# First stage of a six-stage transformer kernel: the order of the next batch's turns and projections among the scan's units

## The reference

```python
# layer 1: linear attention, 16 heads of 32
q, k, v = heads(x @ q_w.T + q_b), heads(x @ k_w.T + k_b), heads(x @ v_w.T + v_b)
qp, kp = elu(q) + 1.0, elu(k) + 1.0
kv = einsum('bhsd,bhse->bhde', kp, v)
z = einsum('bhsd,bhd->bhs', qp, kp.sum(axis=2))[..., None]
attn = einsum('bhsd,bhde->bhse', qp, kv) / (z + EPS)
x = layernorm(x + (attn.reshape(...) @ o_w.T + o_b))
# layer 2: a selective scan over ctx (4 x 512 x 256), gated by silu(x)
u = silu(causal_conv4(einsum('bld,ed->bel', ctx, in_proj_w)) + conv_b)
dt_low, Bm, Cm = split(x_proj_w @ u)              # 16, 16, 16 rows
dt = softplus(dt_proj_w @ dt_low + dt_proj_b)
state = state * exp(dt * A) + (dt * u) * Bm       # 512 steps, 16 states
y = (sum(state * Cm) + D * u) * silu(x)
x = layernorm(x + y)
```

## Time and profile before

| what | value |
|---|---|
| median of 3 runs | 2933.25 us (2930.64 to 2933.45) |
| profiled execution | 2924.15 us |
| its span, first to last instruction | 2922.5 us |
| mean granted clock of PE over the span | 0.947 |
| PE busy | 2622.4 us (90%) |
| DVE busy | 2023.4 us (69%) |
| ACT busy | 1172.5 us (40%) |
| POOL busy | 650.1 us (22%) |
| stage 1 | until about 843 us |

### The profile page before, as it was taken

How to read it: one execution, slowest core, us unless ns; L and a number is a source line. 1 busy time by engine, 2 the same in 40 slices (tenths; PEclk the granted TensorE clock), 3 DMA queues, 4 the chain that set the end, 5 groups by cost and what they waited for, 6 DMA issues and landing times. The chain is left out here.

```text
span 2922.5 us, 29347 instructions
## 1 busy us (share of the span) xinstructions
PE 2622.4 (90%) x9682; PEld 1657.0 (57%) x9682; DVE 2023.4 (69%) x4017; ACT 1172.5 (40%) x2107; POOL 650.1 (22%) x569
## 2 busy tenths in 40 slices
PE   5687897998979889799989999999999998999998
PEld 2233343343448655466656665666666665588886
DVE  2779889789885557688876888578867887222232
ACT  3343363444443222255544555355544555121111
POOL 0544445345411145311101111011101110000000
PEclk9898998999979999899999999999999999999999
DMA  4111112111221102333233223232222314300000
GB/s 143 36 59 51 58 45 79 44 44 65 80 79 58 65 29 87 114 101 101 93 97 114 79 77 91 83 116 75 82 84 89 109 45 127 121 0 30 29 15 15
DMA packets 90785, 212.46 MB, mean 73 GB/s; under 512 B 9990, under 2 KB 34822, under 8 KB 86540
## 3 DMA queue, kind: packets, MB, share of 16 engines
q1 hardware_dynamic: 81324, 178.26, 18.8%
q0 software_dynamic: 5472, 21.01, 1.9%
q10 hardware_dynamic: 3840, 11.34, 1.1%
HBM read 164.11 MB, written 46.47 MB: 72 GB/s over the span
## 5 line engine op out<-in xcount | busy, mean ns | idle before, releaser
L2104 POOL TENSOR_TENSOR h<-du,Bb 128x1024 f32<-128x1024 f32 x128 | 310.2, 2425 | 300.8 <-DVE h L1667 286.9
L1662 DVE TENSOR_TENSOR_SCAN h<-bank,h 128x512 f32<-128x512 f32 x256 | 299.4, 1206 | 25.8 <-ACT bank L1267 18.7
L1267 ACT ACTIVATE bank<-dt,A 128x512 f32<-128x512 f32 x256 | 174.6, 690 | 327.5 <-DVE h L1662 325.0
L1438 ACT ACTIVATE p<-bank,sm,rq 128x512 f32<-128x512 f32 x256 | 199.2, 778 | 243.5 <-DVE sm L2019 243.5
L2182 POOL TENSOR_TENSOR rq<-rq,mhalf 128x4 f32<-128x4 f32 x64 | 69.5, 1085 | 797.0 <-DVE rq L1973 797.0
L637 PE MATMUL bank<-pT,v 128*128 128x512 f32 x512 | 233.0, 598 | 2.8 <-ACT pT L1158 2.8
L251 POOL TENSOR_SCALAR rstd<-mv 128x1 f32<-128x1 f32 x96 | 29.0, 302 | 925.0 <-DVE mv L245 925.0
L637 PE MATMUL bank<-kr,q 128*128 128x512 f32 x512 | 232.9, 598 | 0.0
L837 PE MATMUL bank<-h,ident 128*128 128x512 f32 x256 | 157.3, 699 | 80.6 <-DVE h L1667 80.5
L962 PE MATMUL bank<-x_hi,wxq_s 128*128 128x512 f32 x512 | 189.5, 452 | 6.6 <-DVE x_lo L1994 6.6
L1929 DVE COPY_PREDICATED val<-msk,val 128x258 f32<-128x258 int32 x448 | 173.8, 451 | 28.2 <-DVE val L1929 0.5
(11 more groups left out here) (239 smaller groups left out, 5560.6 us busy)
## 6 DMA issues: line engine op xcount, KB each, us to landing
wxq_s<-wq_dram SPq DMA_DIRECT2D x48, 512.0 KB, 4.4
Bb<-bc_dram SPq DMA_DIRECT2D x32, 512.0 KB, 3.5
Cb<-bc_dram SPq DMA_DIRECT2D x32, 512.0 KB, 3.6
x_dram<-xo POOLq DMA_DIRECT2D x16, 1024.0 KB, 4.7
xc<-x_dram SPq DMA_DIRECT2D x16, 1024.0 KB, 5.3
woh<-in_Wo SPq DMA_DIRECT2D x64, 256.0 KB, 2.6
wxv_s<-wkv_dram SPq DMA_DIRECT2D x12, 1024.0 KB, 5.4
wxk_s<-wkv_dram SPq DMA_DIRECT2D x12, 1024.0 KB, 7.5
```

What stands on the lines that cost most here:

```text
L1267: act.activation(bank[2 + n][:, :], dt[:, c % 2, et, :], ACT.Exp, scale=A[:, et, 2 * w + n:2 * w + n + 1]).then_inc(dA_ready, 1)
L1438: act.activation(p4[:, t, :], bank[4 + t][:, :], ACT.Exp, bias=sm4[:, 4 + t:5 + t], scale=rq[:, hh % 2, 1, t:t + 1], accum_out=sm4[:, 8 + ...
L1662: dve.tensor_tensor_scan(h[:, s, n, :], bank[2 + n][:, :], h[:, s, n, :], 0.0, ALU.mult, ALU.add).then_inc(scanned, 1)
L2104: pool.tensor_tensor(h[:, G % HR, :, :], du[:, et:et + 1, :].to_broadcast([P, 2, S]), Bb[:, w % 2, :, :], ALU.mult).then_inc(dBu_ready, 1)
```

## The change

In stage 1 only:

1. `turn_x` of the next batch moves from slots 30 and 31 to slots 15, 17 and 18, since attended values now stay in `er` (written in place) and no longer take `xT`. The first three `values` of the next batch go to slots 29 to 31, the fourth to slot 1; for batch 0 the first three are computed before the first scan, ahead of `in_xdbl(0)`.
2. `keys` move from slots 3 to 6 to slots 2, 3, 4 and 6; `in_project` goes from two at slot 7 and two at slot 12 to one each at slots 5, 7, 9 and 11, `queries` from slots 13 to 16 to slots 8, 10, 12 and 14. DVE's `conv`, `key`, `query` follow.
3. `keys_values` moves from slot 18 to 13, `in_xdbl` from 17 to 16, `normalisers` from 19 to 17, `turn_normalisers` from 20 to 18, and `in_dt`, `spread`, `attend`, `project_out`, `first`, `last` one slot earlier. POOL's `ln_pool` of the first norm goes from units 30, 31, 0, 1 to units 29, 30, 31, 0.
4. ACT: `value` copies follow the new order (two of them in the n == 0 place of units 0 and 1), `gate_x1` moves from unit 0 of the next batch to unit 31.

```diff
         list0(*[("in", 0, n) for n in range(KI)], *[("x", 0, k) for k in range(KD)], *[("q", 0, n) for n in range(KD)],
-              ("xdbl", 0), *[("dt", 0, n) for n in range(KI)])
+              ("v", 0, 0), ("v", 0, 1), ("v", 0, 2), ("xdbl", 0), *[("dt", 0, n) for n in range(KI)])
...
+            list0(("kv", c, 0), ("kv", c, 1))
+            if c:
+                list0(("q", c, 3))
             if more:
+                list0(("x", c + 1, 0), ("x", c + 1, 1), ("xdbl", c + 1))
+            list0(("z", c))
...
-                group(d[:, :], [(attnT[:, k, t * P:(t + 1) * P], wo[:, k, :]) for k in range(KD)] + [(pick[:, 2, :], rows[:, :])], bank_full)
+                group(d[:, :], [(er[:, k // 2, k % 2, t * P:(t + 1) * P], wo[:, k, :]) for k in range(KD)] + [(pick[:, 2, :], rows[:, :])], bank_full)
...
             for n in range(KD):
                 queries(0, n)
+            pe.wait_ge(rows_ready, START + 1)
+            for t in range(3):
+                values(0, t)
             in_xdbl(0)
...
+                    if U == 1:
+                        values(c, 3)
+                    if U in (2, 3, 4):
+                        keys(c, U - 2)
+                    if U == 6:
+                        keys(c, 3)
+                    if U in (5, 7, 9, 11) and more:
+                        in_project(c + 1, (U - 5) // 2)
+                    if U in (8, 10, 12, 14) and c:
+                        queries(c, (U - 8) // 2)
+                    if U == 13:
+                        keys_values(c)
+                    if U == 15 and more:
+                        turn_x(c + 1, 0)
+                        turn_x(c + 1, 1)
+                    if U == 16 and more:
                         in_xdbl(c + 1)
+                    if U == 17:
+                        normalisers(c)
+                        if more:
+                            turn_x(c + 1, 2)
                     if U == 18:
                         turn_normalisers(c)
+                        if more:
+                            turn_x(c + 1, 3)
...
+                    if U in range(29, 32) and more:
+                        values(c + 1, U - 29)
...
-            gate_x1(B - 1)
+                            if U == 31:
+                                if more:
+                                    value(c + 1, 0)
+                                gate_x1(c)
...
-                    if U in (30, 31):
-                        ln_pool(pool, after(c, 8, U - 30), U % 2)
-                    if U in (0, 1) and c:
-                        ln_pool(pool, after(c - 1, 8, 2 + U), U % 2)
+                    if U in (29, 30, 31):
+                        ln_pool(pool, after(c, 8, U - 29), (U - 29) % 2)
+                    if U == 0 and c:
+                        ln_pool(pool, after(c - 1, 8, 3), 1)
```

More of the change, by code:

```diff
@@ L186, in build @@
             if more:
-                list0(*[("x", c + 1, k) for k in range(KD)])
+                list0(("v", c + 1, 0), ("v", c + 1, 1), ("v", c + 1, 2))
         list0(*[("yt", B - 1, t) for t in range(NT)])
@@ L801, in _ @@
                             pe.matmul(bank[4 + et][:, :], diagD[:, et, :], u[:, et, :], start=True, stop=False)
[L802 to L811, removed]
@@ L831, in _ @@
-                    if U in (30, 31) and more:
-                        turn_x(c + 1, 2 * U - 60)
-                        turn_x(c + 1, 2 * U - 59)
+                        if more:
+                            turn_x(c + 1, 3)
+                    if U in (19, 20) and more:
+                        in_dt(c + 1, 2 * U - 38)
+                        in_dt(c + 1, 2 * U - 37)
+                    if U in (21, 22):
+                        spread(c, 2 * U - 42)
+                        spread(c, 2 * U - 41)
@@ L1190, in key, with value @@
             def key(c, t):
-                if c and t == 0:
-                    act.wait_ge(*FREED["at", c - 1, 2])
-                    act.wait_ge(*FREED["at", c - 1, 3])
                 exp_relu(8 * c + t + (0 if c else 4), ("k", c, t), 0.0, 0.0)
+            def value(c, t):
+                d, free = full("v", c, t)
+                act.activation(va[:, t, :, 0:P], d[:, :].rearrange("p (g e) -> p g e", g=4), ACT.Copy).then_inc(free, 1)
             def gate_u(c):
@@ L1249, in _ @@
             query(0, 3)
+            for t in range(3):
+                value(0, t)
             copy_xdbl(0)
@@ new lines, in _ @@
+                            if U == 19:
+                                d, free = full("zt", c)
+                                act.activation(zr[:, :], d[0:H0, :], ACT.Copy).then_inc(free, 1)
+                                if more:
+                                    turned(c + 1, 3)
+                            if U in (20, 21) and more:
+                                relu_abs(c + 1, 2 * U - 39)
+                            if U in (22, 23) and more:
+                                exp_pair(c + 1, U - 22)
@@ L1290, in _ @@
+                            if U == 24 and more:
                                 plus_one(c + 1, 1)
@@ L1761, in _ @@
                         add_relu(c + 1)
+                    if U in range(26, 30):
+                        first(c, U - 26)
                     if U in range(27, 31):
-                        first(c, U - 27)
-                    if U in range(28, 32):
-                        last(c, U - 28)
+                        last(c, U - 27)
             gated(B - 1)
@@ L2123, in _ @@
                         inputs(c + 1, et)
-            for t in range(2, 8):
+            for t in range(3, 8):
                 ln_pool(pool, after(B - 1, 8, t), t % 2)
```

138 lines of the change are left out of this document (61 added, 77 removed).

## The result

| | before | changed |
|---|---|---|
| median of 4 runs each | 2933.07 us (2930.64 to 2933.45) | 2914.74 us (2913.45 to 2915.19) |
| ratio | | 0.9936 [0.9924, 0.9948] |
| profiled execution, span | 2924.15, 2922.5 us | 2913.45, 2911.4 us |
| first scan starts | 86.0 | 97.4 |
| stage 1 ends (DVE's first row of stage 2) | 843.8 | 822.0 |

A forecast was written before the change was run, and what follows sets the result against it. In stage 1 DVE paces the scan, it and PE waiting by turns, so DVE's waits were priced: 12.1 - 19.2 - 14.6 + 10.4 + 4 - 6.5 - 7.5 = -21.3 us on 2924.15, plus 9.1 to the median: 2912 us, range 2888 to 2938.

The forecast's parts named there:

- first scan: Prologue: three value projections of 4.0 us ahead of `in_xdbl(0)`, uncovered, delay the first scan by 12.1 us.
- waits of `conv`: DVE's waits for in-projections fall from 42.2 to 23 us; only each batch's first `conv` waits, 7 to 8 us.
- `kvb`: DVE's waits for `keys_values`: slot 13 finishes before DVE asks after unit 14, so all 14.6 us go.
- zT: DVE's waits for the normalisers rise from 5.3 to 15.7 us, a loss of 10.4.
- keys: Keys one slot earlier: DVE asks faster than PE supplies, costing some 4 us in batches 0 and 3 together.
- rstd: Batch boundary: DVE's wait for the fourth rstd falls from 9.5 to 3 us, gain 6.5.
- exponentials: DVE's waits for ACT's exponentials fall from 18.7 to some 13.5 us as value copies stop holding up ACT.
- queries and the end: Queries asked for later behind PE, and the last `gate_x1` earlier: gain of about 1 us each.
- one of my signs of being wrong: Stage 1, DVE: waits for in-projections at more than one `conv` would show the forecast wrong.
- nothing to 0.4 us: `gate_x1` in unit 31: ACT's 4.0 us against DVE's unit of 3.57 to 4.2, costing nothing to 0.4 us.
- PE out of the way: Rival, chance 0.17: early values fit PE's boundary idle time, first `conv` waits 3 us, normalisers 1.3; some 2888.
- The slower case: Rival, chance 0.13: PE bounds slots 29 to 5, at half clock behind pauses; 25 to 27 us a batch; 2948.

The follow-up runs named there:

- the second pair: Kernel before and changed kernel, both unedited, run and profiled once more: 2933.13 us and 2915.92 us.
- C: Changed kernel with each batch's fourth value projection moved from slot 1 to behind the second in-projection (slot 7): 2897.56 us, ratio 0.9893.
- F: Changed kernel with in-projections in twos again (slots 5 and 9), queries in slots 10, 11, 12, 14: 2915.48 us, ratio 0.9952.
- G: Changed kernel with all four value projections in slots 7 to 10, none before the first scan, ACT's copies at units 8 to 11: 2921.16 us, ratio 0.9968.
- E: Changed kernel with `keys_values` in slot 14 instead of 13: 2911.66 us, ratio 0.9947.
- B: Changed kernel with the normalisers ahead of the next batch's `in_xdbl`, both at slot 17: 2912.39 us, ratio 0.9943.
- H: Changed kernel with `gate_x1` in unit 0 of the next batch, between its two exponentials: 2915.32 us, ratio 0.9950.
- D: Changed kernel with batch 0's three early values behind the dt projections and the fourth value behind the second in-projection: 2884.14 us, ratio 0.9845.

## Why the prediction was right, and where it was not

Measured by the first profile of each kernel; "again" is the second pair.

| term | forecast | measured |
|---|---|---|
| first scan | +12.1 | +11.4 (again +13.7) |
| waits of `conv` | 42.2 to 23 | to 20.9 |
| `kvb` | 14.6 to 0 | to 0 |
| zT | 5.3 to 15.7 | to 18.9 |
| keys | +4 | +3.9 waiting, +5.7 longer rows |
| rstd | 9.5 to 3 | to 2.5 |
| exponentials | 18.7 to 13.5 | to 10.1 |
| from there to the end of stage 1 | -33.4 | -33.2 (again -28.0) |
| end of stage 1 | -21.3 | -21.8 (again -14.3) |
| median | 2912 | 2914.74 |

- **The method held**, but the closeness is luck: DVE's waits, priced one by one, give the end of stage 1 within a microsecond in one pair of profiles and within 7 us in the other, and misses of up to 5.6 us a term cancel. The six terms behind the first scan measured -21.3, -14.6, +13.6, +9.6, -7.0 and -8.6, in all -28.3; queries' elus add -4.7 (rows 11.6 to 8.2, waits 1.3 to none): -33.0, against 757.8 to 724.6. I had put queries and the end together at 2. The unit's product, some 4.6 us more, and smaller rows cancel. In the normalisers' sum the parts make 15.5, not 15.7.
- **To the median** I kept the distance of 9.1 us of the profiled execution. It is 1.3 for the changed kernel: that profile's untouched stages were long, those of before short. That 2912 lies so near 2914.74 is luck as well. Of the 21.8 us in stage 1 the medians show 18.3, which is inside the interval of the ratio (3.5 us either way).
- **The first `conv`** waits 5.63, 6.12 and 5.36 us (I had 7 and 8 and 8). The count from `gated` was close: the fourth value starts 15.06 us behind it (15.0 forecast), and `conv` 40.2 and 41.9 us behind it in batches 1 and 2 (42.2 forecast). What failed is that such a pause always makes PE slow: after 3.54 us of idle time in batch 1 the value took 3.70 us, after 3.73 in batch 2 5.40, after 2.76 in batch 3 5.24, so the length of the pause alone does not decide it. Nor does the slow row lengthen the wait: in batch 2 a key behind it is late too (0.67 us, and its elu takes 2.40), and DVE asks for `conv` 36.5 us behind `gated`, in batch 1 34.0 (33.9 forecast). C shows that the fourth value's place makes the wait, in batches 1 and 2. In batch 0 I had only the first `conv` late, and it is three: 5.63, 1.17 and 2.59. That was one of my signs of being wrong, and it came.
- **The other in-projections** do alternate with units, but F shows that taking them apart, with the queries' slots that go with it, was worth 5 to 7 us of stage 1: I gave the right gain to the wrong edit. Which edit took away the 21 us of waits for `conv` no single run shows: they stay at 16.9 in F and at 20.8 in G. What G does bring back, in time and under another name, is 21 to 23 us.
- **Keys and values**: I put the 14.6 us down to the early slot and 10.4 back at the normalisers as its price. E refutes the sizes: with the slot one unit later `kvb` waits 1.5 us more and zT 1.2 to 1.9 less. The zT wait is that of two PE projections before one DVE request, as B shows by moving it to ACT. I had 4.2, 5, 5 and 1.3 in the four batches; it is 4.41, 6.20, 6.63 and 1.69. In the longer ones DVE takes 17.8 us from unit 13 to its request (17.7 forecast), and `keys_values` waits for ACT's reading of the third query as I had it (2.40 us), but PE's chain takes 24.0 and 24.4 us in place of 22.6. In batch 2 PE is slow behind that wait (8 matmuls in 1.62 us, 24 in 2.84 before it); in batch 1 it is not (8 in 1.16), but the fourth query waits 0.47 us for DVE and the normalisers take 4.27 in place of 3.6.
- **The keys' term** failed most, 4 for 9.6. I took "DVE's elu is under 0.7 us"; a key that DVE must wait for takes up to 2.55, as the last section shows.
- **The boundary** held: POOL's wait for B fell from 6.30 to 0.23 us. On `gate_x1` the trace decided against the drain that ScalarE: Activation LUTs in the Trainium skill, section What ACT_TABLE_LOAD costs, gives: in the changed kernel the load starts at 272.67 and the exponential at 273.97. H confirms it twice a boundary. It also shows that the silu's place can cost 5 us of waits, which my "nothing to 0.4 us" did not look for; the kernel before had none of them, so they are no part of the 18.7 us of exponentials. Those fell further than forecast.
- **The rivals.** PE out of the way (2888) did not come by itself: the fourth value's bank was held. D gets there (2884), by moving that value and those of the prologue, while zT still waits 20.8 us. The slower case needed 21 us of `conv` and normaliser waits a batch; there are 12 to 14 in each of the first three, and PE's granted clock in them is 0.92 to 0.96, above the 0.89 to 0.91 of the earlier trace rows, not below. The stages behind show no change beyond what three profiles of the kernel before differ by.

## What to carry to other kernels

Where two engines wait for each other by turns, ask of each piece of work which stretch has room for it, not how finely it is cut: four projections put back into the crowded first half of a batch cost 21 to 23 us (with ACT's order as in G), in-projections put together again 5 to 7, a slot later for `keys_values` nothing. In a prologue, put nothing ahead of the chain that the first scan hangs on, if a wait further on would cover it (12 us). And a wait removed by swapping two pieces on one engine may come back under another engine's name; read the sum of the waits, not the one that was aimed at.

## What was not expected of the hardware

An elu of a key, a `TENSOR_TENSOR` on two SBUF operands, takes 0.68 us, but 1.31 to 2.55 us if it begins while POOL's product (also SBUF to SBUF) is running. POOL in the changed kernel:

```profile
117.54 2.36 POOL L2130 TENSOR_TENSOR h<-du,Bb 128x1024 f32<-128x1024 f32 x1 [1.23 <-DVE h L1693]
124.12 2.36 POOL L2130 TENSOR_TENSOR h<-du,Bb 128x1024 f32<-128x1024 f32 x1 [4.23 <-DVE h L1693]
```

and DVE:

```profile
119.13 1.31 DVE L1652 TENSOR_TENSOR kp<-er 128x512 f32<-128x512 f32 x1 [1.74 <-ACT er L1200]
124.90 2.13 DVE L1652 TENSOR_TENSOR kp<-er 128x512 f32<-128x512 f32 x1 [0.94 <-ACT er L1200]
```

POOL's rows end at 119.90 and 126.48, DVE's at 120.44 and 127.03, each 0.54 or 0.55 us behind; so it is for the other two long ones of this kernel, at 501.76 and 691.04. However long the overlap, DVE ends that much behind POOL: by these ends it does not run slower, it stands until POOL is nearly through. By SBUF — State Buffer in the Trainium skill, section SBUF: two separate sides, the pair of ports that the two engines share is held by whichever began first for its whole instruction, if DVE's reads two operands in SBUF and POOL's reads SBUF too; these rows agree. An elu that follows its unit's product at once gets in ahead of POOL (0.68 us rows, in C all sixteen), and then POOL's row reads 2.63 to 2.68 us in place of 2.35; one for which DVE waited 0.5 to 1.7 us finds POOL there. In the second profile of the kernel before a wait of 0.16 us was enough: that elu took 2.88 us. So a short wait of DVE costs more than its length: four waits of 3.9 us brought 5.7 us of longer rows with them.
